# Sharing the last expert blocks of two token halves: 71 slots in place of 78 in a two-layer transformer kernel

## The reference, cut to what matters

```python
# x: (4, 1024, 256) = 32 tiles of 128 tokens; ctx_1024: (4, 64, 256)
x = x + L0_xattn(ctx_1024, layernorm(x))      # memory shift and a strided convolution
x = x + L0_ffn(layernorm(x))                  # shared expert + 2 of 8 routed experts
x = x + L1_xattn(layernorm(x), ctx, ctx)      # 16 heads, 64 keys
x = x + L1_ffn(layernorm(x))                  # 2 of 8 routed experts

def L0_ffn(X):                                # d = 256, h = 128, E = 8, K = 2
    shared = silu(X @ sW1 + sb1) @ sW2 + sb2
    logits = X @ routing_W.T + expert_bias
    top_vals, top_idx = top_k(sqrt(softplus(logits)), 2)
    combine = sum(one_hot(top_idx, 8) * top_vals[..., None], axis=-2)
    y = silu(X @ rW1[e] + rb1[e]) @ rW2[e] + rb2[e]      # for each expert e
    return shared + sum_e combine[:, e] * y[e]
```

## Time and profile before

| | |
|---|---|
| median of 3 runs | 813.52 us |
| the profiled execution's own time | 813.08 us |
| its span (first to last instruction) | 811.2 us |
| PE busy | 750.2 us (92%) |
| DVE, ACT, POOL busy | 536.6, 492.0, 436.1 us |
| chain that ended last: PE, DVE, DMA, ACT | 69%, 13%, 6%, 5% of the span; the waits for `fx` loads alone 4% |
| round 0: first to last store of a result | 141.69 to 188.72 us |
| round 1: first to last store of a result | 203.68 to 253.6 us |

### The profile page before, as it was taken

The page is one execution under the profiler, slowest core; times in us unless marked ns, Lnnn a source line. Parts: engine busy times, 40 slices in busy tenths (PEclk is TensorE's granted clock), DMA queues, the critical chain, the costliest instruction groups (busy, mean ns, idle before and its releaser), DMA issues.

```text
span 811.2 us, 16194 instructions
## 1 busy us (share of the span) xinstructions
PE 750.2 (92%) x4633; PEld 655.0 (81%) x4633; DVE 536.6 (66%) x1422; ACT 492.0 (61%) x1379; POOL 436.1 (54%) x400
## 2 busy tenths in 40 slices
PE   4899998999988799999999999799999999999995
PEld 3645736777766599999989998689999999999994
DVE  5777867752774788888888979676544333356455
ACT  2336845665766688888777795456545445445441
POOL 4000565766677768888545878345651454333251
PEclk9889999999999999999999999999999999999999
DMA  8999997897999942942800634814434434565447
GB/s 243 353 285 317 325 297 266 282 292 213 231 260 255 308 123 36 253 102 27 275 1 2 222 118 140 269 55 132 138 125 145 147 110 145 188 210 170 144 150 266
DMA packets 128745, 154.47 MB, mean 190 GB/s; under 512 B 10875, under 2 KB 118550, under 8 KB 127638
## 3 DMA queue, kind: packets, MB, share of 16 engines
q1 hardware_dynamic: 102896, 112.55, 44.9%
q0 software_dynamic: 18624, 34.29, 16.1%
q10 hardware_dynamic: 7142, 6.59, 2.5%
HBM read 77.39 MB, written 76.00 MB: 189 GB/s over the span
## 4 chain that ended last, share of the span: by engine, by line
PE 69%; DVE 13%; DMA 6%; ACT 5%; issue 4%; DVEq 2%; SPq 1%; ACTq 0%
PE psum L864 22%; PE psum L1179 9%; PE psum L1157 8%; PE psum L1251 7%; PE psum L1256 6%; PE psum L1252 6%; DMA fx<-xs_dram 4%; ACT pr L1564 3%; PE psum L1267 3%; PE psum L1167 3%; PE psum L1230 2%; PE psum L1052 1%; DMA yl_late<-yk_dram 1%; DVE xstats L1765 1%; DVE nmx L2329 1%
## 5 line engine op out<-in xcount | busy, mean ns | idle before, releaser
L774 POOL DMA_INDIRECT yk_dram<-ys,L x52 | 54.5, 1048 | 129.4 <-ACT ys L1656 129.1
L721 POOL DMA_INDIRECT X<-yl_dram,slots_y x64 | 103.5, 1618 | 29.8 <-issue 14.2
L1564 ACT ACTIVATE pr<-psum,nmx 128x64 f32<-128x64 f32 x512 | 108.5, 364 | 16.1 <-DVE nmx L2329 15.8
L693 POOL DMA_INDIRECT xs_dram<-N,slots x64 | 65.9, 1029 | 91.0 <-DVEq L1958 61.1
L1251 PE MATMUL psum<-whi,xTh 128*128 x284 | 104.2, 367 | 3.2 <-ACT xTh L1618 2.4
L2429 DVE TENSOR_TENSOR hs<-psum,hs 128x384 f32<-128x384 f32 x71 | 39.7, 560 | 88.1 <-PE psum L1256 81.4
L1252 PE MATMUL psum<-wlo,xTh 128*128 x284 | 96.0, 338 | 0.0
L762 POOL DMA_INDIRECT xs_dram<-N,slots x64 | 69.4, 1085 | 35.6 <-ACT ys L1656 19.1
L1256 PE MATMUL psum<-whi,xTl 128*128 x284 | 74.1, 342 | 2.2 <-DVE xTl L2452 2.0
L754 POOL TENSOR_TENSOR pr<-pr,sm 128x1024 f32<-128x1024 f32 x30 | 57.2, 1908 | 17.9 <-DVE sm L2336 16.9
L1648 ACT ACTIVATE hs<-psum 128x384 f32<-128x384 f32 x71 | 34.9, 491 | 50.3 <-PE psum L1256 48.4
(11 more groups left out here) (374 smaller groups left out, 2048.5 us busy)
## 6 DMA issues: line engine op xcount, KB each, us to landing
fx<-xs_dram SPq DMA_DIRECT2D x78, 130.0 KB, 3.8
yl_dram<-fy SPq DMA_DIRECT2D x78, 128.0 KB
xs_dram<-fill SPq DMA_DIRECT2D x4, 2340.0 KB, 14.6
xs<-xs_dram SPq DMA_DIRECT2D x71, 130.0 KB, 2.1
wlo<-in_L_ffn_W_dram SPq DMA_DIRECT2D x4, 1536.0 KB, 8.5
xs_dram<-cz SPq DMA_DIRECT2D x1, 5070.0 KB, 22.7
xs_dram<-cz SPq DMA_DIRECT2D x7, 650.0 KB, 6.9
X<-in_x_dram SPq DMA_DIRECT2D x4, 1024.0 KB, 11.8
```

The costliest lines, as they stand in the source:

```text
L693: po.indirect_dma_start(XS, bass.IndirectOffsetOnAxis(ap=slot[k][:, t:t + 1], axis=0), N0[:, t, :], None).then_inc(s[done], 16)
L721: po.indirect_dma_start(X[:, t, :], None, YL[b // 2], bass.IndirectOffsetOnAxis(ap=slot_y[k][:, t:t + 1], axis=0), compute_op=ALU.add).the ...
L774: po.indirect_dma_start(YK, bass.IndirectOffsetOnAxis(ap=yid[:, j:j + 1], axis=0), ys[j % YB], None).then_inc(s[f"y_out{j % YB}"], 16)
L1564: last = act(pr[b][:, S * h:S * h + S], bank[2 * b + h // 8][:, S * (h % 8):S * (h % 8) + S], ACT.Exp, bias=nmx[:, h:h + 1])
```

## The change

The two halves now share one row of 71 slots and one result buffer. The first half's full blocks of an expert come first; at least 32 - 7 = 25 of them are there whatever the tokens are. Then comes one open block for each of the 8 experts, which the second half goes on filling, then the second half's further blocks. Round 0 does slots 0 to 24, round 1 slots 25 to 70 (`ENDS = (0, 25, 71)`). The results of the first half lie in slots 0 to 39 (`LO = 40`), so its gathers wait for these.

```diff
-LS = 2 * LT + E - 1
-LA = LG * LS
+LF = 2 * LT - E + 1
+LR = LF + E
+LO = 2 * LT + E
+LA = 2 * TILES + E - 1
+ENDS = (0, LF, LA)
+HALF = BT // 2
+STATS = {LA - 7: (0, 2), LA - 6: (2, 4)}
+NORMED = {LA - 5: (0, 1), LA - 4: (2, 3), LA - 3: (4,), LA - 2: (5,), LA - 1: (6, 7)}
-BREAK, SLOTS = 4, 5
+BREAK, SLOTS = 4, 3
...
 # SP, PE, ACT and DVE, routed(g)
-                first, last = LS * g, LS * g + LS
+                first, last = ENDS[g], ENDS[g + 1]
...
 # POOL
             def collect(b, k, t0, t1):
+                first_in, second_in = ("l_ga", "l_gh"), ("l_gb", "l_gd")
                 if k:
-                    po.wait_ge(s["l_ga"], 16 * BT * (b + 1))
+                    po.wait_ge(s[first_in[t0 % BT // HALF]], 16 * HALF * (b + 1))
                     if b:
-                        po.wait_ge(s["l_gb"], 16 * BT * b)
+                        po.wait_ge(s["l_gb"], 16 * HALF * b)
+                        po.wait_ge(s["l_gd"], 16 * HALF * b)
...
             def routed_done(g):
                 po.wait_ge(s["l_xu"], LQ * (g + 1))
                 for b in range(YB):
-                    po.wait_ge(s[f"ys_out{b}"], routed_out(b, LS * (g + 1)))
+                    po.wait_ge(s[f"ys_out{b}"], routed_out(b, (LO, LA)[g]))
...
             routed_done(0)
             for b in range(2):
-                for k in range(2):
-                    collect(b, k, b * BT, b * BT + BT)
+                collect(b, 0, b * BT, b * BT + BT)
+                for t in (b * BT, b * BT + HALF):
+                    collect(b, 1, t, t + HALF)
...
 # DVE, routed(1): the norm of tiles 0 to 3 alone, on the last seven slots
-                    if g and i == 0:
-                        ve.wait_ge(s["l_gb"], 16 * BT)
-                    if g and 0 <= i < BT:
-                        row_stats(X, i, i + 1)
-                    if g and BT <= i < BT + 8:
-                        first_norm(i - BT)
+                    if j == min(STATS):
+                        ve.wait_ge(s["l_gb"], 16 * HALF)
+                    if j in STATS:
+                        row_stats(X, *STATS[j])
+                    for part in NORMED.get(j, ()):
+                        first_norm(part)
...
 # DVE, attention: the norm of tiles 4 to 7
                 def between(n):
+                    if n == 0:
+                        routed_norm(0, 1)
+                        chain(0, ((HALF, BT),), 1)
+                    if n == 1:
+                        chain(1, ((HALF, BT),), 1)
+                        ve.drain()
+                        chain(2, ((HALF, BT),), 1)
                     if n in (1, 2):
                         routed_norm(1, n - 1)
```

More of the change, by code:

```diff
@@ L299, in build @@
         bank = [psum[:, k, :] for k in range(8)]
-        XS = nc.dram_tensor("xs_dram", [LA * P, XW], F32).ap()
+        XS = nc.dram_tensor("xs_dram", [FILLED * P, XW], F32).ap()
         XS1 = XS.rearrange("r (w a) -> (r w) a", a=1)
-        YL = [nc.dram_tensor(f"yl_dram{g}", [LS * P, D], F32).ap() for g in range(LG)]
+        YL = nc.dram_tensor("yl_dram", [LA * P, D], F32).ap()
         YK = nc.dram_tensor("yk_dram", [2 * ROWS + YB * P, D], F32).ap()
@@ L420, in _ @@
             zeros = zero4[:, :].rearrange("p (a d) -> p a d", a=1)
-            rows_of = [XS[LS * P * g:LS * P * (g + 1), :].rearrange("(p r) d -> p r d", p=P) for g in range(LG)]
-            parts = [LS * i // PAIRS for i in range(PAIRS + 1)]
+            rows_of = [XS[a * P:b * P, :].rearrange("(p r) d -> p r d", p=P) for a, b in ((0, LO), (LO, LA))]
+            parts = [(LA - LO) * i // PAIRS for i in range(PAIRS + 1)]
             sp.wait_ge(s["kvo_in"], 16 * 3)
@@ L1041, in routed @@
             def routed(g):
-                first, last_ = LS * g, LS * g + LS
+                first, last_ = ENDS[g], ENDS[g + 1]
                 def xpose(j):
@@ L1892, in scores, with places @@
                             row_stats(N0, t, t + BT)
-            def places(n, cols, prefix, totals, tot_, inc_, cm, heads, base, nslots, at, t0, done):
+            def places(g):
+                n, cols = LT, E * LT
                 e3 = "p (e t) -> p e t"
+                prefix, totals = (bank[4][:, 256 + 128 * k:256 + 128 * k + cols] for k in range(2))
+                tot_, inc_ = (tc_[:, cols * k:cols * k + cols] for k in range(2))
                 ta_, tb_ = ta[:, 0:cols], tb[:, 0:cols]
+                ta3, tb3 = ta_.rearrange(e3, e=E), tb_.rearrange(e3, e=E)
+                last_t = inc_.rearrange(e3, e=E)[:, :, n - 1:n]
+                last = last_t.rearrange("p e a -> p (e a)")
+                past, delta, start, grow, upto, jump = (ta[:, cols + 32 + E * k:cols + 32 + E * k + E] for k in range(6))
+                nslots, at = (LR, LA - LR)[g], (0, LR)[g]
+                number, e_at = slotno[:, at:at + nslots], eid_f[:, 0:nslots]
+                behind, part = (tb[:, cols + 64 * k:cols + 64 * k + nslots] for k in range(2))
+                cm = wk12[:, 0:nslots * E].rearrange("p (j e) -> p j e", e=E)
@@ L1906, in places @@
[L1906 to L1914, removed]
@@ L1923, in places @@
                 ve.drain()
[L1924 to L1925 removed]
+                nc.vector.tensor_copy(slots[:, :, n * g:n * g + n], hot2[:, :, 0:n])
+                nc.vector.tensor_copy(slots_y[:, :, n * g:n * g + n], hot2[:, :, 0:n])
                 ve.drain()
[L1927 to L1928 removed]
             def choose(g):
@@ L1974, in routed @@
                     ve.drain()
-                for j in range(LS * g, LS * g + LS):
-                    if j == LS * g or j % 4 == 0:
+                first = ENDS[g]
+                for j in range(first, ENDS[g + 1]):
+                    if j == first or j % 4 == 0:
                         experts_of, loaded = four_experts(mybir.EngineType.DVE, j), j
```

106 lines of the change are left out of this document (77 added, 29 removed).

## The result

| | before | after |
|---|---|---|
| median | 812.46 us (811.26 to 814.69, 4 runs) | 823.89 us (823.24 to 824.97, 4 runs) |
| profiled execution: its time, its span | 813.08, 811.2 us | 823.42, 821.6 us |
| PE, DVE, ACT, POOL busy | 750.2, 536.6, 492.0, 436.1 us | 743.9, 541.2, 484.5, 433.9 us |

The kernel before has one run more here than in the table ahead of the prediction. The ratio is 1.0152, with a 95% interval of [1.0126, 1.0178]: slower by 11.4 us, where 824.6 us and "slower" were forecast. PE has 6.3 us less work and the kernel takes 10.4 us more in the profiled executions, so the loss lies in waits.

A forecast was written before the change was run, and what follows sets the result against it. PE, busy 92%, bounds the kernel, with POOL's list behind the rounds hardly waiting. The 7 saved slots are used up by 3.5 and 6.7 us; 813.08 + 11.0 (late `scale(2)`) + 0.5 (restart) = 824.6 us, range 815 to 830.

The forecast's parts named there:

- The slots: In the two rounds: 7 slots fewer at 1.24 to 1.31 us remove 9 us of PE and DMA time.
- Place-finding: On DVE ahead of each round: 12 and 9 more instructions cost 1.4 and 2.1 us, 3.5 in all.
- The sends hold up round 1: Between the rounds: loads need all of POOL's sends, so round 1 begins at 193.3, PE standing 6.7 us.
- The first gather: On POOL in round 1: it waits for slots 0 to 39 and starts at 215.3, 24.0 us later.
- POOL's list: From first gather to `scale(2)`: 81.3 us of POOL's work, so `scale(2)` starts 12.0 us later and 11.0 reach PE.
- The halves: In POOL's gathers: halves of four tiles remove the two landing waits, saving up to 7.3 us.
- the time of 821: If gathers moved out of the round got cheaper by a descriptor-writing rule, up to 4 us, the time would be 821.
- The restart: PE after its longer idle time in the attention: 0.5 us added, with 0 and 2 as bounds.
- Rival 1: Sends don't hold round 1, which starts at 186.6; `scale(2)` at 289.9, time 818; chance 0.20.
- Rival 2: POOL's list isn't what PE waits for; only the rounds count: no change, 813; chance 0.12.
- rival 3: Loads are ready when PE is and gathers cost 1.55 us; round 1 ends 7 us earlier: 806; chance 0.06.
- rival 4: Place-finding 6.7, sends and loads at long ends, 1.24 a slot before the gathers, cold restart 2: 832; chance 0.04.

The follow-up runs named there:

- +8 slots: Changed kernel with POOL's first gathers waiting for slots 0 to 47 instead of 0 to 39: 850.24 us against 839.21 us for the changed kernel.
- gate gone: Changed kernel with the gathers of batches 0 and 1 reading `xs_dram` rows, not waiting for slots' results: 833.45 us, 1.0048 of the kernel before.
- The pair on one chip with the same `SCALED`: Changed kernel and kernel before, both with softmax divisions of tiles 2 to 4 on DVE instead of POOL (`SCALED = 5`): 837.14 us and 835.34 us.

## Why the prediction was right

The likeliest case happened, with its mechanism in its place, and the two runs that move the gate (+8 slots: +1.3%; gate gone: -0.8 to -0.9%) show it to be the cause of about two thirds of the loss. The prediction put all of it there, since its rounds came out even; they did not quite, and the sizes below met in part by luck. Step by step, on the profiled executions:

- **A lead that no step accounts for.** The changed kernel's execution is 3.2 us ahead at the first copy of `choose(0)` (71.12 for 74.34). The new place-finding comes only behind this copy. In the 11 traces of the changed kernel and its variants this copy begins anywhere from 70.73 to 74.44, so single executions differ by as much before DVE reaches anything new. The times below contain this lead. Counted from that copy, the first gather comes 28.4 us later than before, not 25.2, where 24.0 was forecast.

- **The slots** were given their full price of 9 us, and this was used up ahead of the attention, as forecast: the last store of round 1 begins at 255.8 against 253.6 before. The forecast had 253.3, 2.5 us too early, and all of that lies behind slot 39: the last 31 slots took (255.8 - 212.8) / 31 = 1.39 us each instead of 1.31. There a gather starts every 1.87 us, where the round before had 23 in 49.9 us; that fits, but no run tests it. This end, 2.2 us late, is a loss that the sum didn't have.
- **Place-finding**, 3.5 us forecast. By the timeline of DVE `choose(0)` takes 6.75 us from its copy out of PSUM to `slots_y` (71.12 to 77.87), where the earlier trace rows show 4.96; the second takes 6.87 (126.83 to 133.70) for 4.98. Together 3.7 us, right. The first send of the second half came only 0.5 us later (138.18 for 137.66), because of the lead. The pair on one chip with the same `SCALED` has 3.55 us for it.
- **The sends hold up round 1.** PE's pause of 5.20 us was forecast as 6.7. The last send came at 181.88 for 184.4 (it inherits the lead), and the loads landed in 4.5 us in the middle for 5.8. That is one profile of one chip. On the three others round 0 itself stretched until no pause was left; the begin of round 1 gained as little there (6.0 us for 14 slots), but by another way than this step says. Whether `vraw` matters stays open.
- **The first gather**, 216.51 for 215.3: right as the sum of errors. Round 1 began 3.2 us earlier than forecast (mostly the lead), but its first store came 5.5 us after its start instead of 3.3, at half speed, and the next 14 slots took 1.22 us each instead of 1.15, all of which is one wait of PE of 1.22 us for an `fx` load (206.53). So slot 39 was stored at 212.78, where 212.7 was forecast. The landing was the step that missed: 3.73 us from this store to the gather, not 2.6. The 2.6 was read at the end of a round; amid the round, in the other two profiles of the changed kernel, it is 3.45 and 3.53.
- **POOL's list** was forecast at 81.3 us and took 78.0 (216.51 to 294.47): 31 steps of 1.865 us instead of 1.89 make 0.8 of the difference, and the rest of the list, 2.5 us shorter than in the sum, makes the larger part. The gathers behind the round are no cheaper than those within it (most take 1.54 or 1.55 us in both), so the time of 821 that the prediction names for that case did not come. `scale(2)` was late by 9.9 us, not 12.0.
- **The halves** did away with the two landing waits, but for 0.58 us. Their worth was put too low: up to 7.3 us in the sum, 12 us in the run without them, as the second landing wait is 10.55 us there and DVE waits for gathers too. For the same reason the waits for DVE were not all covered in the changed kernel itself: DVE stood 2.26 us at 274.71 until gathers had landed, which the wait at tile 2 then hid.
- **The restart** was given 0.5 us with 2 as its bound; it took the 2. The tile after the wait needed 306.37 - 297.02 = 9.35 us, where 7.4 are usual. Here the errors of the last two terms meet: 9.6 + 2.0 for 11.0 + 0.5.
- **Rival 1** (no hold-up, 818): PE's pause of 5.20 us speaks against it on the first chip. **Rival 2** fell with the two runs on the gate, **rival 3** with the run without it: 1.005 of the kernel before, not 0.99. Of rival 4 the cold restart came, and nearly its 1.24 us a slot ahead of the gathers (1.22); not its place-finding, sends and loads.

## What to carry over

Fewer blocks of work can be worth nothing if a consumer has to wait for a block that now comes later. Here 39 of 78 slots had to be ready before the second engine's list could start; now it is 40 of 71, and the list starts 25 us later, while it had 12.6 us of waits in it. So for each merged block ask first who reads it, then when that reader's list must start so that its last item is in time, and count the slack on the list, not on the busy shares. Moving items of such a list later pays only up to the next place that needs them: gathers put off by two steps too many gave 8 us back at the norm of batch 3.

## What was not expected of the hardware

- After an idle time of 5 to 7 us PE works at half its clock for a while. The stretch behind the pause of 5.20 us, and the one behind the wait of 7.13 us:

```profile
190.20:194.90 4.70, 4.61 (x19) 3.85 (x20) 4.00 (x9) 0.73 (x2) 0.00 (x0) 0.50 0.41 139
297.02:300.50 3.48, 3.48 (x13) 3.09 (x14) 0.84 (x2) 1.08 (x2) 3.38 (x3) 0.50 1.11 332
```

  Both are at a granted clock of 0.50, the level of 1.2 GHz. That a wait of 7 us costs 2 more behind it was seen as a bound and not believed. Shorter waits do it too: in the kernel before, 269.9 to 273.9, some 2 us behind a wait of 2.75 us for DVE, is at 0.57, and a pair of logits products takes 1.05 us there for 0.62.

- The same program takes 812.46, 829.08, 831.24 and 829.73 us (medians), the last three on three chips and the first by all signs on a fourth. Part of the difference stands in round 0: 1.25 us a slot on the first, 1.47 on another, in the kernel before (there with `SCALED = 5`, which touches only the attention). The ratio of the two kernels hardly moved (1.0152, 1.0141, 1.0141).
